# When SyncE waits for scatter-adds: ahead of all loads of a batch, or only ahead of the load of x

## The chip, the cores and the metric

The kernel runs on one core of one Trainium2 chip. The metric is the device time of one execution in microseconds (us); the time given for the kernel before is the median of three runs.

## The reference

One layer of a graph network over 100,000 nodes with 64 features and 25,000 edges:

```python
h = jnp.maximum(_layernorm(x), 0.0)
# src, dst: the two ends of each edge
msgs_f = mlp2(concat[h[src], h[dst], edge_attr], W1_f, b1_f, W2_f, b2_f)
agg    = segment_sum(msgs_f, dst)
msgs_r = mlp2(concat[h[dst], h[src], edge_attr], W1_r, b1_r, W2_r, b2_r)
agg    = agg + segment_sum(msgs_r, src)
out    = x + h + mlp2(concat[agg, h], Wn1, bn1, Wn2, bn2)
```

`mlp2` is two linear layers with a relu between them.

## The kernel before

Everything is float32. A table in device memory holds, for each node, the 128 values ahead of the node network's relu. Three stages work on it.

The first stage (to about 310 us) runs over 98 windows of 1024 nodes: it loads x, normalizes, multiplies by the lower part of Wn1 and stores the rows of the table. Meanwhile GpSimd (POOL) gathers rows of x for the ends of the edges, so that half of all gathers are done ahead of the second stage.

The second stage (about 340 to 1353 us) is the one that the change touches. It runs over 98 batches of 256 edges. A batch has four "tiles" of 128 edge ends. In its step n, each engine does this:

- DVE (`batch`, L1023): `aim` for batch n-2 (L1000, it writes the row numbers `scatter_at`, and first waits until the scatter-adds of batch n-4, which read the same buffer, have landed); `centre` for n+1; `match` for n-1 (L967, it compares `others`, the node numbers of all ends of the batch, with `ids`, and so finds ends that meet in the same node); `normal` for n; `targets` and `messages` for n-1; `add_h` for window n-1 (L1036, x + h).
- PE (`batch`, L850): `join` of n-2 (it sums messages of one node), `turn` of n (transposes `h_ends` and `edge_in`), `layer2` of n-1, `layer1` of n.
- ACT: root, relu, square, `copy_sums` of n-2 (the sums to `to_send`), and h of a window of nodes.
- POOL (`batch`, L570): `scatter` (L518) issues four indirect DMAs of 128 rows, which add `to_send` to rows of the table. It first waits until those of the batch before have landed. Then `gather_odd` (L535) issues two gathers of rows of x for a later batch.
- SyncE (SP, `batch`, L445): `behind_scatter` (L439) waits until the scatter-adds of batch n-4 have landed, the same landing on which `aim` waits. `load` (L353) loads `edge_in` (64 KB of edge features, L364) and twice `others` (128 KB each, the numbers spread to all partitions, L367) of batch n. It waits for its own buffers, `s_turn` and `s_same`, that is for `turn` and `match` of batch n-2. `load_x_edge` (L402) loads 256 KB of x for window n+2 (L385), and `store_xh` (L431) stores x + h of window n-1 (256 KB, L391), after waiting for DVE's `add_h` of that window.

Not all windows are stored: `in_ring` (L296) keeps some in SBUF. In each four windows, one is kept in the first 24 windows and two are kept after that, up to window 95; SP's step then ends with the load of x.

SP's queue runs in order, so whatever stands behind a wait waits as well. `behind_scatter` guards no buffer: it sets when SP's loads are issued. `s_loads_held` is a count on which nobody waits.

The third stage (to the end) loads the table and x + h, runs the rest of the node network and stores the output. It begins when all scatter-adds have landed.

Of the kernel before, what the change touches and what calls it, by code (L numbers as in the profile page):

```python
# [77 lines left out]
def gnn_layer(nc, x, src, dst, edge_attr, W1_f, b1_f, W2_f, b2_f, W1_r, b1_r, W2_r, b2_r, Wn1, bn1, Wn2, bn2, out):  # L78
# [39 lines left out]
    with ExitStack() as ctx:  # L118
# [205 lines left out]
        def _(sp):  # L324
# [106 lines left out]
            def store_xh(w, k):  # L431
                if not w.there(k) or not in_ring(w, k):
                    return
                i, s = w.of(2, k)
                sp.wait_ge(e_xh[s], i + 1)
                place = w.of(NRING, k)[1]
                store_window(out, i, s, flat(nxh[place]), e_stored[place])
# [5 lines left out]
                    sp.sem_inc(s_loads_held, 1)  # L443

            def batch(w):  # L445
                w.do(behind_scatter)
                if w.least() >= 2:
                    w.do(load)
                w.do(load_x_edge, 2, ring=NRING)
                store_xh(w, -1)  # L450

            run(sp, NB, [(4, MORE_FROM * NRING, 4), (MORE_FROM * NRING, 92, 4)], 1, batch)


# [710 lines left out]
```

## Time and profile before

| | us |
|---|---|
| median of the runs (1625.42 to 1633.73) | 1631.61 |
| the profiled execution | 1627.22 |
| its span, first to last instruction | 1625.5 |
| busy in the span: PE, PE weight loads, DVE | 1318.5, 997.1, 972.4 |
| busy in the span: ACT, POOL | 944.0, 1120.1 |
| POOL's scatter-adds, L532, 392 instructions | 640.9 |
| mean granted TensorE clock | 0.835 of full |

Times of instructions are those of the profiled execution. PE is TensorE's matmuls, PEld its weight loads, SPq the queue of SyncE, which only issues DMAs here. "Busy" of a POOL indirect DMA is the time in which POOL makes its descriptors; the data moves afterwards. The queue q0 (software dynamic) carries POOL's DMAs and q1 (hardware dynamic) those of SP; both run on the same 16 DMA engines.

### The profile page before, as it was taken

Reading aid. Unit: us, or ns where it says so; the run is one execution under the profiler, and the core shown is the slowest. Engines: PE = TensorE matmul, PEld = TensorE weight load, DVE = VectorE, ACT = ScalarE, POOL = GpSimd, SP = SyncE. Lnnn points to the kernel's source line nnn. Section 1 sums busy time; section 2 is a strip of 40 time slices with the busy share of each in tenths; the row PEclk is TensorE's granted clock in tenths of the full one; section 3 lists DMA queues with packets and bytes.
Section 4 is the critical chain, followed back from the end, with each engine's and each line's share of the span. In section 5 each row is a group of like instructions: output and inputs, shape, how many; then the busy total and the mean of one; then the engine's idle time right before and its main releaser. Section 6 shows DMA issues by size and latency. Waiting matters only on the chain.

```text
span 1625.5 us, 29085 instructions
## 1 busy us (share of the span) xinstructions
PE 1318.5 (81%) x7070; PEld 997.1 (61%) x7070; DVE 972.4 (60%) x2902; ACT 944.0 (58%) x2256; POOL 1120.1 (69%) x1003
## 2 busy tenths in 40 slices
PE   6988998457787788887877887878888865899998
PEld 4777776345565666665656665656666654666665
DVE  7999998336666666666665666666666641222222
ACT  5888888244555455555545555455555533677776
POOL 7899878888888888888888888888888862000000
PEclk9999999567878777778787778787777777999999
DMA  7999998335555555555545555555555546999998
GB/s 222 310 312 315 315 312 280 101 59 108 103 109 108 107 104 103 102 103 103 102 93 99 101 103 102 98 100 102 103 103 102 102 76 205 333 369 348 346 349 292
DMA packets 238374, 280.71 MB, mean 173 GB/s; under 512 B 53170, under 2 KB 155200, under 8 KB 238348
## 3 DMA queue, kind: packets, MB, share of 16 engines
q1 hardware_dynamic: 168408, 241.57, 44.7%
q0 software_dynamic: 68992, 38.59, 20.3%
q10 hardware_dynamic: 948, 0.30, 0.1%
q14 instruction: 21, 0.17, 0.0%
q8 instruction: 5, 0.08, 0.0%
HBM read 162.62 MB, written 117.72 MB: 172 GB/s over the span
## 4 chain that ended last, share of the span: by engine, by line
POOL 28%; issue 19%; DMA 15%; PE 9%; DVE 5%; ACT 1%; POOLq 0%; SPq 0%; DVEq 0%; another core or an unknown queue 0%; ACTq 0%
POOL table L532 24%; DMA out_x<-ncentred 12%; POOL got_odd L514 5%; DMA table<-to_send,scatter_at 3%; PE bank L846 3%; DVE ncentred L1137 2%; PE bank L820 2%; PE bank L818 2%; PE bank L833 1%; DVE same L979 1%; PE bank L871 1%; DMA same<-table 1%; PE bank L804 1%; PE bank L882 0%; DVE sums L961 0%
## 5 line engine op out<-in xcount | busy, mean ns | idle before, releaser
L532 POOL DMA_INDIRECT table<-to_send,scatter_at x392 | 640.9, 1635 | 134.1 <-issue 118.3
L846 PEld LDWEIGHTS bank<-message,same 128*128 128x128 f32 x1960 | 300.1, 243 | 47.1 <-issue 43.6
L846 PE MATMUL bank<-message,same 128*128 128x128 f32 x1960 | 322.4, 335 | 3.3 <-DVE message L1010 3.3
L639 ACT ACTIVATE nh<-nx,all_sums,all_rstd 128x64 f32<-128x64 f32 x784 | 280.2, 434 | 0.0
L514 POOL DMA_INDIRECT got_even<-in_x,gather_first x196 | 211.8, 1081 | 40.9 <-issue 36.1
L775 PE MATMUL bank<-wn_h,nturned 128*128 128x256 f32 x784 | 196.6, 394 | 26.9 <-ACT nhidden L683 18.4
L514 POOL DMA_INDIRECT got_odd<-in_x,gather_at x180 | 179.9, 999 | 54.8 <-issue 54.2
L818 PE MATMUL bank<-turned,w_ends 128*128 128x256 f32 x392 | 175.5, 540 | 37.8 <-ACT turned_edge L609 37.1
L804 PE MATMUL bank<-ident,h_ends 128*128 128x128 f32 x196 | 51.4, 355 | 184.4 <-DVE h_ends L1019 181.4
L1004 DVE TENSOR_TENSOR scatter_at<-moved,ids 128x4 int32<-128x4 f32 x98 | 16.0, 163 | 296.6 <-DMA table<-to_send,scatter_at 296.6
L775 PEld LDWEIGHTS bank<-wn_h,nturned 128*128 128x128 f32 x784 | 143.1, 192 | 63.3 <-issue 33.0
L820 PE MATMUL bank<-turned_edge,w_edge 64*128 64x256 f32 x392 | 179.4, 547 | 0.0
L991 DVE CUSTOM_DVE_ANT_0 junk<-same,earlier 128x128 bf16<-128x128 f32 (+3 forms) x392 | 168.9, 487 | 0.0
L713 ACT ACTIVATE nhidden<-bank,bn_col 128x512 f32<-128x512 f32 x196 | 124.0, 684 | 70.2 <-PE bank L871 70.2
L616 ACT ACTIVATE hidden<-bank,b 128x256 f32<-128x256 f32 x196 | 82.1, 470 | 124.3 <-PE bank L820 122.4
L979 DVE TENSOR_SCALAR same<-others,ids 128x128 f32<-128x128 int32 (+3 forms) x392 | 143.7, 429 | 11.7 <-issue 7.6
L804 PEld LDWEIGHTS bank<-ident,h_ends 128*128 128x128 f32 x196 | 28.9, 181 | 195.3 <-issue 195.3
L871 PE MATMUL bank<-ident,same 128*128 128x128 f32 x784 | 108.4, 282 | 38.1 <-DMA same<-table 36.5
L833 PE MATMUL bank<-w2n,hidden 128*128 128x128 f32 x784 | 139.0, 336 | 0.0
L625 ACT COPY to_send<-bank 128x512 f32<-128x512 f32 x98 | 56.6, 577 | 139.4 <-PE bank L846 55.7
L871 PEld LDWEIGHTS bank<-ident,same 128*128 128x128 f32 x784 | 85.4, 143 | 77.5 <-issue 53.7
L820 PEld LDWEIGHTS bank<-turned_edge,w_edge 64*128 64x128 f32 x392 | 75.1, 239 | 94.0 <-issue 94.0
(78 smaller groups left out, 1971.0 us busy)
## 6 DMA issues: line engine op xcount, KB each, us to landing
nx<-in_x SPq DMA_DIRECT2D x194, 256.0 KB
table<-nhidden SPq DMA_DIRECT2D x97, 512.0 KB
same<-table SPq DMA_DIRECT2D x97, 512.0 KB, 5.3
others<-numbers SPq DMA_DIRECT2D x196, 128.0 KB
out_x<-ncentred SPq DMA_DIRECT2D x97, 256.0 KB, 4.4
nx<-out_x SPq DMA_DIRECT2D x55, 256.0 KB, 4.6
out_x<-nh SPq DMA_DIRECT2D x31, 256.0 KB
table<-to_send,scatter_at POOLq DMA_INDIRECT x392
```

The lines of the kernel that those rows point to most:

```text
L514: pool.indirect_dma_start(to[:, k * D:(k + 1) * D], None, x, bass.IndirectOffsetOnAxis(ap=numbers[:, k:k + 1], axis=0)).then_inc(landed, 16)
L532: pool.indirect_dma_start(table, bass.IndirectOffsetOnAxis(ap=scatter_at[s][:, k:k + 1], axis=0), to_send[s][:, k, :], None, compute_op=AL ...
L639: last = act.activation(nh[s][:, g, :], nx[place][:, g, :], ACT.Relu, bias=all_sums[:, at, g:g + 1].rearrange("p a g -> p (a g)"), scale=a ...
L713: act.activation(nhidden[s][:, odd * 512:odd * 512 + 512], bank[2 + 2 * s + odd][:, :], ACT.Relu, bias=bn1_col[:, 0:1]).then_inc(n_hidden[ ...
L775: last = pe.matmul(bank[2 + 2 * s + half][:, c:c + 2 * M], nturned[s][:, q * P:(q + 1) * P], wn1_h[:, :, :].rearrange("p a m -> p (a m)"), ...
L818: pe.matmul(bank[2 + s][:, c:c + JT * P], w1_ends[:, end, :], turned[s][:, 0:JT * P], start=True, stop=False)
L820: last = pe.matmul(bank[2 + s][:, c:c + JT * P], w1_edge[:, end, :], turned_edge[s][:, :], start=False, stop=True)
L833: last = pe.matmul(bank[4 + s][:, k * M:(k + 1) * M], hidden[s][:, end, j * P:(j + 1) * P], w2n[:, end, :], start=True, stop=True)
L846: last = pe.matmul(bank[6 + s][:, k * M:(k + 1) * M], same[s][:, o, k * P:(k + 1) * P], message[s][:, o, :], start=(o == k), stop=(o == KB ...
L871: last = pe.transpose(bank[2 + 2 * s + odd][:, q * P:(q + 1) * P], ntab[place][:, g * M:(g + 1) * M], ident[:, :])
L979: last = dve.tensor_scalar(same[s][:, o, 0:w], row[:, 0:w], ids[s][:, o:o + 1], None, ALU.is_equal)
L991: last = dve.tensor_tensor_reduce(junk[s][:, k, 0:w], same[s][:, k, 0:w], earlier[:, KB * P - w:], 1.0, 0.0, ALU.mult, ALU.add, before[s][ ...
```

## The change

In SP's `batch` the wait for the landing changes its place with `load`. Nothing else changes.

```diff
             def batch(w):
-                w.do(behind_scatter)
                 if w.least() >= 2:
                     w.do(load)
+                w.do(behind_scatter)
                 w.do(load_x_edge, 2, ring=NRING)
                 store_xh(w, -1)
```

## Rows read from the trace of the kernel before

**Rows 1.** Busy time by stretch of the second stage; the columns are in the heading.
```profile
core 0: us, PE busy (x) PEld busy (x) DVE busy (x) ACT busy (x) POOL busy (x), PEclk, DMA share, GB/s
500.00:700.00 200.00, 163.13 (x773) 123.88 (x771) 126.51 (x454) 103.19 (x291) 164.96 (x116) 0.76 0.55 104
900.00:1100.00 200.00, 161.36 (x769) 122.27 (x768) 125.63 (x448) 101.86 (x288) 164.64 (x117) 0.77 0.54 101
```

**Rows 2.** Groups from 351.28 to 1295.70 us, 91 steps; busy, mean ns | idle before.
```profile
L532 POOL DMA_INDIRECT table<-to_send,scatter_at x364 | 595.8, 1637 | 111.3 <-issue 110.1 <-ACT to_send L625 1.2
L514 POOL DMA_INDIRECT got_odd<-in_x,gather_at x180 | 179.9, 999 | 54.8 <-issue 54.2 <-DMA table<-to_send,scatter_at 0.6
L1004 DVE TENSOR_TENSOR scatter_at<-moved,ids 128x4 int32<-128x4 f32 x92 | 15.1, 164 | 280.1 <-DMA table<-to_send,scatter_at 280.1
```

**Rows 3.** Timeline of a step with a store: start, us, engine, line.
```profile
797.06 0.10 SPq L364 DMA_DIRECT2D edge_in<-in_edge_attr  x1
797.75 1.75 POOL L532 DMA_INDIRECT table<-to_send,scatter_at  x1 [0.30 <-issue]
798.53 0.77 SPq L367 DMA_DIRECT2D others<-numbers  x2
799.38 0.35 SPq L385 DMA_DIRECT2D nx<-in_x  x1
802.55 0.68 DVE L1048 TENSOR_TENSOR nsquares<-nx,nh 128x512 f32<-128x512 f32 x1
803.26 0.37 SPq L391 DMA_DIRECT2D out_x<-nsquares  x1
803.58 1.55 POOL L532 DMA_INDIRECT table<-to_send,scatter_at  x1 [0.30 <-issue]
806.99 0.16 DVE L1004 TENSOR_TENSOR scatter_at<-moved,ids 128x4 int32<-128x4 f32 x1 [3.42 <-DMA table<-to_send,scatter_at]
808.05 1.75 POOL L532 DMA_INDIRECT table<-to_send,scatter_at  x1 [0.30 <-issue]
```

**Rows 4.** DMA queues from 805.13 to 806.50: packets, MB, share of 16 engines.
```profile
q0 software_dynamic: 141, 0.06, 53.8%
q1 hardware_dynamic: 16, 0.01, 2.4%
```

**Rows 5.** The same queues from 799.50 to 801.75.
```profile
q1 hardware_dynamic: 450, 0.28, 48.7%
q0 software_dynamic: 105, 0.05, 23.0%
```

**Rows 6.** Timeline of the step whose store came late.
```profile
409.10 1.57 POOL L532 DMA_INDIRECT table<-to_send,scatter_at  x1 [0.30 <-issue]
409.50 0.68 DVE L1048 TENSOR_TENSOR nh<-nx,nh 128x512 f32<-128x512 f32 x1
410.37 0.37 SPq L391 DMA_DIRECT2D out_x<-nh  x1
413.04 0.17 DVE L1004 TENSOR_TENSOR scatter_at<-moved,ids 128x4 int32<-128x4 f32 x1 [2.53 <-DMA table<-to_send,scatter_at]
413.94 1.75 POOL L532 DMA_INDIRECT table<-to_send,scatter_at  x1 [0.68 <-issue]
```

**Rows 7.** DMA queues from 411.00 to 412.75.
```profile
q1 hardware_dynamic: 144, 0.26, 45.2%
q0 software_dynamic: 152, 0.08, 42.1%
```

**Rows 8.** Stores of x + h by SP, count and first and last start.
```profile
L391 SPq DMA_DIRECT2D out_x<-nh x31: 343/368/374, 294.5 to 1321.6; - x31
L391 SPq DMA_DIRECT2D out_x<-nsquares x24: 356/368/376, 352.6 to 1301.3; - x24
```

**Rows 9.** Timeline without gathers, near the end of the stage.
```profile
1304.72 0.16 DVE L1004 TENSOR_TENSOR scatter_at<-moved,ids 128x4 int32<-128x4 f32 x1 [3.12 <-DMA table<-to_send,scatter_at]
1305.50 1.77 POOL L532 DMA_INDIRECT table<-to_send,scatter_at  x1 [2.54 <-DMA table<-to_send,scatter_at]
```

**Rows 10.** Timeline of a step in which DVE's L1048 and the fourth scatter-add meet.
```profile
824.27 0.68 DVE L1048 TENSOR_TENSOR nh<-nx,nh 128x512 f32<-128x512 f32 x1
824.39 2.00 POOL L532 DMA_INDIRECT table<-to_send,scatter_at  x1 [0.30 <-issue]
```

**Rows 11.** SP's queue: waits, us in total, times, longest; then who waits for `edge_in`.
```profile
SPq L443 <- DMA table<-to_send,scatter_at: 224.2, 42, 8.4
  ACT turned L608: 84.2, 53
  PEld bank L804: 52.0, 17
```

## The prediction

> **What bounds the kernel now.** I read the busy times by stretch first. In the second stage POOL is busy 165 of each 200 us, a little more than PE, which runs there at a granted clock of 0.76 [rows 1]. Busy shares that close decide nothing, so the groups come next. In the 91 steps from 351.28 to 1295.70 us (944.4 us, so 10.38 us a step) POOL has 364 scatter-adds of 1.637 us and 182 gathers of about 1.0 us, and its idle time ahead of them is nearly all "issue", the fixed 0.30 us between two instructions; only 1.8 us of it is a wait for anybody [rows 2]. So 4 x (1.64 + 0.30) + 2 x (1.00 + 0.30) = 10.4 us is the step: POOL runs through without a stop and sets the pace. PE and DVE have gaps; DVE alone stands 280 us in `aim`, waiting for scatter-adds to land [rows 2]. SP waits for the same landing [rows 11], but nobody on the path waits for SP: DVE has no wait for `others` among its costly ones, and the waits behind PE's `edge_in` transposes [rows 11] lie on ACT and PE, which have slack against POOL.
>
> The timeline of one step then shows how thin POOL's cover is. The fourth scatter-add is issued at 803.58 and its descriptors are made at 805.13; two gathers follow; DVE sees the landing at 806.99, that is 1.86 us later; the next batch's first scatter-add, which needs that landing, starts at 808.05, 2.92 us after 805.13 [rows 3]. The gap of 1.06 us between landing and start looks like slack, but most of it is not: where no gathers stand between, POOL starts 0.78 us after DVE's `aim` (1304.72 to 1305.50) [rows 9]. So the real slack is 1.06 - 0.78 = about 0.3 us a step. That is the number on which the change hangs.
>
> **The change part by part.** No instruction is added or removed. In each step three DMAs (64 + 2 x 128 KB) move in SP's queue from behind the wait for the landing to ahead of it. What then releases them is the end of SP's step before and the waits for their own buffers.
>
> *Steps behind a step without a store.* SP's step ends with the load of x, right after a landing; the edge loads then wait for `match` of two batches ago, which DVE does some 2.5 us after its `aim`. They go out while the first scatter-adds are made, where in the kernel before the load of x went (799.38) [rows 3]. The load of x goes out some 2.3 us earlier, at once after the landing. The fourth scatter-add, whose landing counts, moves alone as before. Cost: 0; what hides it is that landings of the first three scatter-adds are waited for only through the fourth.
>
> *Steps behind a store.* Here `turn` and `match` of the batch two back have long been done when SP gets past the store, which itself waited for DVE's L1048. In the kernel before SP stored at 803.26 and was then silent until 807.40 or so, after the landing; now it goes on to issue the edge loads at some 803.7 to 805.3. The store's 0.3 us ahead of the fourth scatter-add is typical: in the step shown, SP's store stands at 803.26 against 803.58 [rows 3]; over the stage the difference goes from -0.4 to +1.3 us with a median near 0. So the edge loads fall on the time in which the fourth scatter-add's data moves. Before, that time was empty: from 805.13 to 806.50 q0 moves 141 packets and q1 only 16 [rows 4]. I found q1 in that window in one step of 92.
>
> What does it cost to fill it? That one step is the nearest row. The store was issued at 410.37, late, and its 144 packets moved together with the fourth scatter-add, at 45% and 42% of the engines [rows 7]. The descriptors were made at 409.10 + 1.57 = 410.67 and the landing came at 413.04, 2.37 us later, against about 1.77 in the other steps (1.86 in rows 3): +0.6 us. And POOL's next scatter-add has an idle time of 0.68 instead of 0.30 us: +0.38 us on the path [rows 6]. That agrees with 0.6 - 0.3 of slack. The other end is the first scatter-add of a step, beside which the edge loads themselves move now: from 799.50, the end of its descriptors, to 801.75, 2.25 us, only 105 packets of q0 are through while q1 has 450 [rows 5], where the undisturbed fourth had 141 in 1.37 us [rows 4]. So edge loads, with many small packets (96 or more per us), hold a scatter-add up by over 0.9 us if they meet it whole; that would be 0.9 - 0.3 = 0.6 to 0.7 us of stall a step. The lower end: if the edge loads' data comes late (in rows 3 `others` is issued 1.5 us after `edge_in`), they meet only the tail, the delay stays under 0.3 us and costs nothing. I take the +0.38 us of the one step measured: the transfer is different but the meeting, a SP transfer over the fourth scatter-add, is the same, and the size lies between the ends.
>
> How often: 55 stores [rows 8], less those ahead of the first scatter-adds and the last two, behind which no edge loads come, leaves about 50. So 50 x 0.38 = 19 us, with ends 0 and 50 x 0.7 = 35 us.
>
> *DVE's phase.* DVE's step hangs on the landing, POOL's now in part too, so DVE shifts by 0.3 us against POOL in steps behind a delayed landing. POOL is sensitive to this: L1048 that ends 0.35 us ahead of the fourth scatter-add leaves it at 1.55 us [rows 3]; one that begins 0.12 us ahead of it makes it 2.00 us [rows 10]; one that begins 0.40 us behind it leaves it at 1.57 us [rows 6]. In the 92 steps, 25 fourth scatter-adds are long by over 0.1 us, 8.6 us together. A shift of 0.3 us takes some out and puts others in. The first scatter-add is 1.75 us where DVE's comparison starts after it and 1.64 where before, 0.1 us more in the shifted steps. I take 0.1 us a step, 50 x 0.1 = 5 us, with ends -9 (all 25 freed) and +20 (50 x 0.4).
>
> The Trainium skill speaks on both sides here. Its page "DMA: Bandwidth & Descriptors", section "Queues, rings and completion order", has each DMA engine take turns between the queues it has work for, a packet at a time; by that rule 45% against 42% is what two queues with work get, and the trace agrees [rows 7]. The same page's "Rules for kernel authors" advise to issue a DMA early and wait late, since its fixed cost then overlaps; by that rule the change is free or better, and the time stays at 1631 us. The rows on POOL's slack bear against it. On the phase, the page "SBUF — State Buffer", section "SBUF: two separate sides", says that a DVE instruction with two SBUF inputs and a GpSimd instruction exclude each other for a shared port pair, whichever starts first; rows 6 and 10 agree, L1048 having two SBUF inputs.
>
> Sum: 19 + 5 = 24 us. The profiled execution's 1627.2 would become 1651; the median of the runs shown is 4.4 us above it, so 1631.6 + 24 = 1655.6, say 1655 us. Differences under 0.5% (8 us) can't be told from no change.
>
> **The rivals.**
> - *Hidden after all.* The edge loads come so late or move so thinly that the landing slips by less than 0.3 us; the gathers cover it. For it: q1's `others` packets move at a third to a half of the engines' time, and half of the steps aren't touched. Against it: rows 5. Time 1628 to 1637, about 1632.
> - *Full meeting.* The landing slips by 0.9 us or more, as rows 5 show for the first scatter-add, and DVE's shift puts L1048 onto the fourth one: 50 x (0.65 + 0.3) = 47, up to 1631.6 + 47 = 1679.
> - *Faster, by phase.* The landing slips by less than 0.3 us, POOL loses nothing, and DVE's L1048, which in 25 steps begins up to 0.3 us ahead of the fourth scatter-add, moves behind its start, as in rows 6. Decides from: a shift of over 0.1 to 0.3 us in those steps without the clean ones moving in. Price: at most 8.6 us, 1623. Against it: most clean steps have L1048 ending within 0.4 us ahead of that start, so they'd move in.
> - *It doesn't do what it says.* The buffers' own waits hold the edge loads as long as the landing did. In no step as long by the timeline: behind a store `match` was done some 5 us before, and in the others the hold ends some 7 us ahead of the next landing. It would give 1631, inside the first rival.
>
> **How the numbers follow.** Forecast (a meeting at the size of rows 6, 1640 to 1666): 0.55. Full meeting, 1666 to 1680: 0.18. Hidden: 0.21. Faster by phase, 0.06, of which half is over 8 us. So slower 0.74, same 0.23, faster 0.03. The range leaves out the faster case and the ends of the others: 1630 to 1676.
>
> **What would show it.** In the changed trace: the edge loads of half of the steps within 0.5 us behind a store, with q1 busy while the fourth scatter-add moves; the time from the fourth scatter-add's end to DVE's L1004 2.3 to 2.7 us in those steps and 1.8 in the others; POOL's idle ahead of its first scatter-add 0.6 to 0.9 us in them, so a wait "DMA table" or "issue" that grows by 15 to 35 us over the stage; steps of 10.8 and 10.3 us in turn; first and third stage unchanged. Wrong would be: landings at 1.8 us everywhere (then it is hidden), or slower with landings unchanged (then DVE's phase alone did it). The steadiness of the meeting is what could fail: SP's place against POOL depends on DVE, and DVE on PE's clock.

## The result and the profile after

| | before | after |
|---|---|---|
| median of the runs, us | 1629.58 (1625.42 to 1633.73) | 1661.72 (1658.86 to 1670.3) |
| the profiled execution, us | 1627.22 | 1662.97 |
| its span, us | 1625.5 | 1661.2 |
| mean granted TensorE clock | 0.835 | 0.836 |

The changed kernel is slower, by a ratio of 1.0206 with a 95% interval of 1.0158 to 1.0254, or 32 us. All of it lies in the second stage: from POOL's first scatter-add to its last it takes 35 us more in the profiled executions. POOL carries the loss. Two groups of the changed kernel's page (busy us, mean ns | idle us ahead of them, what ended most of it):

```profile
L532 POOL DMA_INDIRECT table<-to_send,scatter_at x392 | 651.8, 1663 | 158.0 <-issue 122.8
L514 POOL DMA_INDIRECT got_odd<-in_x,gather_at x180 | 179.9, 999 | 54.9 <-issue 54.9
```

The same two groups of the kernel before, on its page:

```profile
L532 POOL DMA_INDIRECT table<-to_send,scatter_at x392 | 640.9, 1635 | 134.1 <-issue 118.3
L514 POOL DMA_INDIRECT got_odd<-in_x,gather_at x180 | 179.9, 999 | 54.8 <-issue 54.2
```

The gathers are the same. The scatter-adds have 158.0 - 134.1 = 23.9 us more idle time ahead of them and take 651.8 - 640.9 = 10.9 us longer; together 34.8 us, against 35.7 us by which the span grew. So two rows of a page account for the loss: two thirds are waits, one third longer instructions.

The changed kernel's busy times by stretch, to set beside [rows 1]:

```profile
core 0: us, PE busy (x) PEld busy (x) DVE busy (x) ACT busy (x) POOL busy (x), PEclk, DMA share, GB/s
500.00:700.00 200.00, 149.66 (x744) 115.18 (x743) 122.50 (x441) 98.83 (x278) 160.52 (x112) 0.79 0.56 103
900.00:1100.00 200.00, 160.93 (x760) 122.63 (x760) 122.02 (x438) 100.39 (x283) 162.78 (x114) 0.76 0.55 99
```

112 instead of 116 POOL instructions fit into the first of these stretches, and no engine is busier there than before: the sign of a pace-setting engine that now waits. The granted clock of TensorE went from 0.76 to 0.79 in the first stretch and from 0.77 to 0.76 in the second, so it isn't the cause.

Where POOL waits, a step with a store shows (timeline of the changed kernel: start, us, engine, line):

```profile
669.26 0.37 SPq L391 DMA_DIRECT2D out_x<-nh  x1
669.46 1.57 POOL L532 DMA_INDIRECT table<-to_send,scatter_at  x1 [0.30 <-issue]
669.88 0.39 SPq L364 DMA_DIRECT2D edge_in<-in_edge_attr  x1
670.45 0.96 SPq L367 DMA_DIRECT2D others<-numbers  x2
672.65 0.98 POOL L514 DMA_INDIRECT got_odd<-in_x,gather_at  x1 [0.30 <-issue]
674.59 0.17 DVE L1004 TENSOR_TENSOR scatter_at<-moved,ids 128x4 int32<-128x4 f32 x1 [5.19 <-DMA table<-to_send,scatter_at]
674.84 0.35 SPq L385 DMA_DIRECT2D nx<-in_x  x1
675.42 1.76 POOL L532 DMA_INDIRECT table<-to_send,scatter_at  x1 [1.78 <-DMA table<-to_send,scatter_at]
```

It answers to [rows 3]. The edge loads go out 0.6 us behind the store, while POOL still makes the descriptors of the fourth scatter-add (ready at 669.46 + 1.57 = 671.03). DVE sees the landing 3.56 us after that, not 1.86, and POOL's next scatter-add stands 1.78 us instead of 0.30. The DMA queues of the changed kernel in the stretch from 671.64 to 673.00, while that scatter-add's data moves:

```profile
q1 hardware_dynamic: 238, 0.11, 30.8%
q0 software_dynamic: 49, 0.02, 26.5%
```

In the same length of time q0 had moved 141 packets undisturbed [rows 4]; beside 238 packets of SP's it moves 49. From the point of the step at which [rows 4] begin, the end of the descriptors, the contrast is larger: from 671.03 to 672.40 q1 moves 405 packets and q0 only 6.

The meeting isn't the same in each step. A step of the changed kernel with a milder one:

```profile
733.64 0.68 DVE L1048 TENSOR_TENSOR nsquares<-nx,nh 128x512 f32<-128x512 f32 x1
733.68 2.07 POOL L532 DMA_INDIRECT table<-to_send,scatter_at  x1 [0.30 <-issue]
734.36 0.37 SPq L391 DMA_DIRECT2D out_x<-nsquares  x1
735.45 0.39 SPq L364 DMA_DIRECT2D edge_in<-in_edge_attr  x1
736.03 0.95 SPq L367 DMA_DIRECT2D others<-numbers  x2
737.78 0.16 DVE L1004 TENSOR_TENSOR scatter_at<-moved,ids 128x4 int32<-128x4 f32 x1 [3.12 <-DMA table<-to_send,scatter_at]
738.67 1.67 POOL L532 DMA_INDIRECT table<-to_send,scatter_at  x1 [0.30 <-issue]
```

Here the store comes 0.68 us behind the start of the fourth scatter-add, the edge loads 1.1 us behind the store, and the landing only 2.03 us behind the descriptors; POOL doesn't wait. But the scatter-add itself takes 2.07 us, since L1048 began 0.04 us ahead of it.

I worked the averages out from such rows of the timeline, for 90 steps. The first of them begins at 350.74 us and the last at 1305.54 us in the changed kernel, at 351.28 and 1275.32 us in the one before. "Landing" is from the end of the fourth scatter-add's descriptors to DVE's L1004; "next start" is from the same point to POOL's next scatter-add.

| mean over steps, us | landing | next start | step |
|---|---|---|---|
| before, 50 with a store | 1.75 | 2.92 | 10.43 |
| before, 40 without | 1.78 | 2.91 | 10.32 |
| after, 50 with a store | 2.49 | 3.36 | 10.92 |
| after, 40 without | 1.85 | 2.93 | 10.52 |

The 50 steps with a store fall into kinds. In 19 the store is issued earlier than 0.2 us behind the start of the fourth scatter-add: the landing takes 3.03 us on average and the next start 3.87. In the 31 others the landing takes 2.16 us on average. In all, 29 of the 50 stand longer than before and 21 don't. The 90 steps are 32.5 us longer: 22.5 us in the time to the next start and 10 us in longer scatter-adds (33 instead of 25 fourth ones are long by over 0.1 us, and the first and third ones are a little longer on average).

### The profile page after: what moved, and what is told of

Read it like the earlier page. It is cut to its first block, busy times and chain, and to the rows that moved or that the text cites. A ratio compares the mean times of both kernels' runs of the same rounds, so it can differ in the third digit from the quotient of the medians.

```text
span 1661.2 us, 29085 instructions
## 1 busy us (share of the span) xinstructions
PE 1313.0 (79%) x7070; PEld 995.4 (60%) x7070; DVE 972.3 (59%) x2902; ACT 945.0 (57%) x2256; POOL 1131.1 (68%) x1003
## 4 chain that ended last, share of the span: by engine, by line
POOL 35%; issue 21%; DMA 17%; PE 3%; DVE 2%; POOLq 0%; SPq 0%; ACT 0%; DVEq 0%
POOL table L532 28%; DMA out_x<-ncentred 11%; POOL got_odd L514 6%; DMA table<-to_send,scatter_at 5%; DVE ncentred L1137 2%; PE bank L871 1%; PE bank L882 1%; PE bank L846 1%; DMA same<-table 1%; PE bank L892 0%; SPq L391 0%; PE bank L820 0%; PE bank L818 0%; PE bank L833 0%; DVE same L979 0%
## 5 line engine op out<-in xcount | busy, mean ns | idle before, releaser
L532 POOL DMA_INDIRECT table<-to_send,scatter_at x392 | 651.8, 1663 | 158.0 <-issue 122.8
L846 PEld LDWEIGHTS bank<-message,same 128*128 128x128 f32 x1960 | 286.4, 234 | 47.0 <-issue 41.4
L846 PE MATMUL bank<-message,same 128*128 128x128 f32 x1960 | 308.1, 325 | 5.4 <-DVE message L1010 5.4
L804 PE MATMUL bank<-ident,h_ends 128*128 128x128 f32 x196 | 55.7, 380 | 223.2 <-DVE h_ends L1019 218.1
L1004 DVE TENSOR_TENSOR scatter_at<-moved,ids 128x4 int32<-128x4 f32 x98 | 16.0, 163 | 313.8 <-DMA table<-to_send,scatter_at 313.8
L818 PE MATMUL bank<-turned,w_ends 128*128 128x256 f32 x392 | 170.0, 524 | 23.0 <-ACT turned_edge L609 23.0
L820 PE MATMUL bank<-turned_edge,w_edge 64*128 64x256 f32 x392 | 171.2, 524 | 0.0
L833 PE MATMUL bank<-w2n,hidden 128*128 128x128 f32 x784 | 147.2, 350 | 0.0
L833 PEld LDWEIGHTS bank<-w2n,hidden 128*128 128x128 f32 x784 | 139.3, 266 | 2.2
```

The costliest lines, as they stand in the source:

```text
L532: pool.indirect_dma_start(table, bass.IndirectOffsetOnAxis(ap=scatter_at[s][:, k:k + 1], axis=0), to_send[s][:, k, :], None, compute_op=AL ...
L818: pe.matmul(bank[2 + s][:, c:c + JT * P], w1_ends[:, end, :], turned[s][:, 0:JT * P], start=True, stop=False)
L820: last = pe.matmul(bank[2 + s][:, c:c + JT * P], w1_edge[:, end, :], turned_edge[s][:, :], start=False, stop=True)
L833: last = pe.matmul(bank[4 + s][:, k * M:(k + 1) * M], hidden[s][:, end, j * P:(j + 1) * P], w2n[:, end, :], start=True, stop=True)
L846: last = pe.matmul(bank[6 + s][:, k * M:(k + 1) * M], same[s][:, o, k * P:(k + 1) * P], message[s][:, o, :], start=(o == k), stop=(o == KB ...
```

## The experiments

Theory 1 is the meeting: edge loads that follow a store move while the fourth scatter-add does, it lands late, and POOL waits. Theory 2 is the phase: only DVE's place against POOL has changed. Theory 3 blames the load of x, which now goes out directly behind the landing.

**The change in half of the steps.** `e1_behind_no_store` loads ahead of the wait only where the step of SP before ended without a store:

```diff
+                early = w.there(-2) and not in_ring(w, -2)
+                if early:
+                    w.do(load)
                 w.do(behind_scatter)
-                if w.least() >= 2:
+                if w.least() >= 2 and not early:
                     w.do(load)
```

> The edge loads go ahead of the wait for the landing only in steps of SP that follow a step without a store (42 of 92); behind a store the order is the old one. Theory 1 (meeting: edge loads that follow a store run over the data of the fourth scatter-add, it lands late and POOL waits): no meeting is left, so the time is that of the kernel before, 1629 us within 8, with DVE's row L1004 1.75 to 1.85 us behind the end of the fourth scatter-add in all steps. Theory 2 (phase: only DVE's place against POOL has changed, by the new order of the loads, and long scatter-adds make the loss): part of the loss stays, some 40 of 90 steps, +10 to +15 us. Theory 3 (the load of x, which now goes out 2.3 us earlier, is what hurts): it goes out early in the steps touched, so about half of the loss, +15 us.

Measured: 1629.54 us, ratio 0.9997 (0.9979 to 1.0015): no loss, with a mean landing of 1.8 us in both kinds of step. `e2_behind_store` is the same without the `not`:

> The other half: the edge loads go ahead of the wait only in steps of SP that follow a store (50 of 92). Theory 1 (meeting): the whole loss of the changed kernel, +25 to +35 us, so 1655 to 1665; the landing behind a store 2.5 us after the fourth scatter-add on average against 1.8. Theory 2 (phase) and theory 3 (early load of x): about half of it, +15 us.

Measured: 1658.51 us, ratio 1.0176 (1.0151 to 1.0201): nearly the whole loss, with a mean landing of 2.41 us behind a store. The groups of POOL's scatter-adds, first of `e1_behind_no_store`:

```profile
L535 POOL DMA_INDIRECT table<-to_send,scatter_at x392 | 642.7, 1640 | 134.5 <-issue 118.4 <-DMA table<-to_send,scatter_at 15.1 <-ACT to_send L628 0.9
```

and of `e2_behind_store`:

```profile
L535 POOL DMA_INDIRECT table<-to_send,scatter_at x392 | 654.3, 1669 | 154.5 <-issue 121.0 <-DMA table<-to_send,scatter_at 33.5
```

The first has nearly the idle time and the busy time of the kernel before, the second nearly those of the changed one. Theory 3 would have split the loss, and theory 2 had put 10 to 15 us on the first of the two; neither came. The phase has a price, as `e6_before_add_first` will show, but this change reaches it only by way of late landings.

**The change without the meeting.** `e3_store_late` keeps the changed order in every step, and holds the store back behind the next landing:

```diff
                 w.do(load_x_edge, 2, ring=NRING)
-                store_xh(w, -1)
+                store_xh(w, -2)
```

(with one more step at the end of the loop).

> The changed kernel, with each store of x + h held back one step further: it is issued behind the load of x of the next step, so behind the landing. SP's step then ends with something that is never later than the landing plus 1 us in every step, and the edge loads of all steps wait for the comparison of two batches ago, some 2.5 us behind the landing. Theory 1 (meeting): nothing of SP moves while the fourth scatter-add does; landings at 1.8 us, time 1629 us within 8, so the whole loss is gone though the edge loads still go ahead of the wait in every step. Theory 3 (the load of x goes out at once behind the landing): the loss stays, about 1660. Theory 2 (phase): anything between, with landings unchanged.

Measured: 1628.29 us, ratio 0.9988 (0.9973 to 1.0003). The loss is gone with the load of x still directly behind the landing. A step of `e3_store_late`:

```profile
695.29 0.37 SPq L364 DMA_DIRECT2D edge_in<-in_edge_attr  x1
695.83 0.94 SPq L367 DMA_DIRECT2D others<-numbers  x2
699.24 1.57 POOL L532 DMA_INDIRECT table<-to_send,scatter_at  x1 [0.31 <-issue]
702.49 0.16 DVE L1004 TENSOR_TENSOR scatter_at<-moved,ids 128x4 int32<-128x4 f32 x1 [3.12 <-DMA table<-to_send,scatter_at]
702.72 0.34 SPq L385 DMA_DIRECT2D nx<-in_x  x1
703.76 0.72 SPq L391 DMA_DIRECT2D out_x<-nh  x1
```

The edge loads are 4 us ahead of the fourth scatter-add, and the landing comes 1.68 us behind its descriptors.

**Which of the loads.** `load` is split into `load_features` (`edge_in`) and `load_numbers` (both `others`), and only one goes ahead of the wait. `e4_features_ahead`:

```diff
                 if w.least() >= 2:
-                    w.do(load)
+                    w.do(load_features)
                 w.do(behind_scatter)
+                if w.least() >= 2:
+                    w.do(load_numbers)
```

> Only edge_in, the 64 KB of edge features (256 packets), goes ahead of the wait; both loads of others (512 packets, 256 KB) stay behind it. Theory 1 (meeting): edge_in alone holds the engines for some 0.3 us behind the store; it delays the landing behind a store by 0.1 to 0.3 us, which POOL's 0.3 us of slack mostly covers: 1630 to 1640 us. Theory 2 and 3: theory 3 expects no loss here, since the load of x stays as late as before; theory 2 expects up to +8 us either way with landings at 1.8 us.

Measured: 1630.18 us, ratio 1.0005 (0.9992 to 1.0018), with a mean landing of 1.87 us behind a store. `e5_numbers_ahead` has the two in the other order:

> Only others, the two loads of 128 KB (512 packets), go ahead of the wait; the load of edge_in stays behind it. Behind a store, others now moves some 0.6 us sooner after the store than in the changed kernel. Theory 1 (meeting): others are what holds the fourth scatter-add up, so most of the loss of the changed kernel or all of it is there, +20 to +40 us, landings of 2.3 to 3.5 us behind a store. Rival 4 (it takes the number of SP's DMAs, or all 320 KB): about a half, +10 to +15 us.

Measured: 1691.61 us, ratio 1.0376 (1.0353 to 1.04): 62 us lost, beyond the expectation of theory 1 (up to 40), and twice the loss of the change itself. Moving less ahead cost more. Without `edge_in` in front, `others` is issued 1.33 us behind the start of the fourth scatter-add on average, not 1.80, and in 49 of the 50 steps POOL's next start is late, not in 29: the mean landing behind a store is 2.99 us, the next start 3.82 us. The group of the scatter-adds in `e5_numbers_ahead`:

```profile
L539 POOL DMA_INDIRECT table<-to_send,scatter_at x392 | 656.4, 1675 | 180.5 <-issue 115.5 <-DMA table<-to_send,scatter_at 63.8 <-ACT to_send L632 1.2
```

**DVE's phase, and the meeting made whole.** DVE's `add_h` (L1048) goes ahead of `messages`, so that it no longer waits for PE; the store comes about 1 us sooner. `e6_before_add_first` does this to the kernel before:

```diff
-                w.do(messages, -1)
                 add_h(w, -1)
+                w.do(messages, -1)
```

> The kernel before, with DVE's add_h ahead of messages in each step, so that L1048 doesn't wait for PE and begins behind the start of the third scatter-add and ends ahead of the fourth; SP's store comes about 1 us earlier. Theory 1 says nothing new here: no edge loads meet the landing, it stays at 1.8 us. Theory 2 (phase) puts its price: the 25 long fourth scatter-adds (8.6 us in all) go, so 1620 to 1629 us; if the third one gets long instead, it is the same as before.

Measured: 1619.12 us, ratio 0.9939 (0.9919 to 0.9958). A step of `e6_before_add_first`:

```profile
632.48 1.56 POOL L532 DMA_INDIRECT table<-to_send,scatter_at  x1 [0.30 <-issue]
632.65 0.69 DVE L1048 TENSOR_TENSOR nsquares<-nx,nh 128x512 f32<-128x512 f32 x1
633.37 0.37 SPq L391 DMA_DIRECT2D out_x<-nsquares  x1
634.34 1.55 POOL L532 DMA_INDIRECT table<-to_send,scatter_at  x1 [0.30 <-issue]
```

L1048 begins 0.17 us behind the start of the third scatter-add, which stays at 1.56 us, and has ended a microsecond ahead of the fourth. None of the 90 fourth ones is long any more. In the profiled executions all scatter-adds together are 6.3 us shorter than in the kernel before; the rest of the 10 us is not traced to a row. `e7_after_add_first` is the same edit on the changed kernel:

> The changed kernel, with the same move of add_h. The store, and with it the edge loads behind it, comes about 1 us earlier against the fourth scatter-add, so the edge loads meet it whole in every step behind a store. Theory 1 (meeting): every such landing is like the worst ones of the changed kernel, 3.0 to 3.5 us, POOL stands 0.8 to 1.3 us more in 50 steps: 1670 to 1695 us. Theory 2 (phase: long fourth scatter-adds make the loss): the loss gets smaller, 1625 to 1650 us.

Measured: 1677.85 us, ratio 1.0291 (1.0271 to 1.0311). This separates the two theories best: the edit that makes the kernel before 10 us faster makes the changed kernel 16 us slower. The group of `e7_after_add_first` from its page:

```profile
L532 POOL DMA_INDIRECT table<-to_send,scatter_at x392 | 637.6, 1627 | 187.1 <-issue 122.4
```

Its scatter-adds are 14.2 us shorter than in the changed kernel, its idle time ahead of them is 29.1 us longer. The store now comes early in every step, and so do the edge loads; the landings behind a store take 2.74 to 3.49 us. In the changed kernel itself 9 of the 50 took over 3.13 us, the longest 3.87 us, so the delay hangs on where in the scatter-add's time the loads fall, and this kernel's mean isn't its upper bound.

`e8_both` puts `add_h` first in `e3_store_late`:

> The changed kernel with the store held back behind the next landing, as in e3_store_late, and add_h ahead of messages. Theory 1: no SP transfer near the fourth scatter-add and no long fourth ones, so as e6_before_add_first or a little better: 1618 to 1628 us, a version that is faster than both kernels. Rival: the long ones move to the third scatter-add, 1629 us.

Measured: 1621.28 us, ratio 0.9946 (0.9929 to 0.9964). It is 0.5% faster than the kernel before, which is clear of noise, like `e6_before_add_first`, and not better than that one: the early edge loads bring nothing of their own.

**What sets the size of the delay.** Three kernels put different loads ahead of the wait, all with `add_h` first, so that the meeting comes early in each step behind a store. `e9_x_ahead_add_first`:

```diff
+                w.do(load_x_edge, 2, ring=NRING)
                 w.do(behind_scatter)
                 if w.least() >= 2:
                     w.do(load)
-                w.do(load_x_edge, 2, ring=NRING)
```

> As e6_before_add_first, but the load of x (256 KB in 128 packets of 2 KB) goes ahead of the wait for the landing and the edge loads stay behind it. Behind a store it meets the fourth scatter-add whole. The question is what sets the size of the delay. If it is the bytes or the time that the engines need (256 KB, about 0.8 us of all 16 engines, near to that of both others), the landing is 1.2 us late as in e5 and e7, and the time is 1665 to 1680 us. If it is the number of packets, it is about a half or less: landing 0.5 to 0.6 us late as in rows 6, POOL stands some 0.3 us in 50 steps, 1632 to 1642 us.

Measured: 1636.89 us, ratio 1.0048 (1.0032 to 1.0064), or 18 us above `e6_before_add_first`, the kernel to compare it with, since both have `add_h` first. `e10_one_number_add_first` splits `load_numbers` by end (`load_one` is the first of the two loads, `load_rest` is `edge_in` and the second):

```diff
-                    w.do(load)
+                    w.do(load_one)
                 w.do(behind_scatter)
+                if w.least() >= 2:
+                    w.do(load_rest)
```

> As e6_before_add_first, but one of the two loads of others (128 KB in 256 packets) goes ahead of the wait, the other and edge_in stay behind it. By the number of packets: half of the delay of both, landing 0.6 to 0.7 us late, 1635 to 1645 us. By a fixed price of any load with such packets that meets the scatter-add: as with both, 1665 us or more.

Measured: 1637.89 us, ratio 1.005 (1.0037 to 1.0064), 19 us above `e6_before_add_first`. `e11_both_numbers_add_first` is `e5_numbers_ahead` with the edit of `add_h`:

> As e5_numbers_ahead with add_h ahead of messages: both loads of others (256 KB in 512 packets) ahead of the wait, edge_in behind it, the meeting as early as it gets. The whole-meeting price for 512 packets: landing 3.0 to 3.3 us, 1670 to 1682 us. It would be less only if they now pass ahead of the scatter-add's data in part: then landing below 2.8 us, 1650 to 1665 us.

Measured: 1665.1 us, ratio 1.021 (1.0173 to 1.0246); the landing of 2.86 us is between the two cases expected, and the time is at the edge of the lower one. Means over the steps with a store, worked out as above:

| ahead of the wait, `add_h` first | KB, packets | landing, us | next start, us |
|---|---|---|---|
| nothing (`e6_before_add_first`) | 0 | 1.75 | 2.92 |
| x (`e9_x_ahead_add_first`) | 256, 128 | 2.31 | 3.13 |
| one of `others` (`e10_one_number_add_first`) | 128, 256 | 2.30 | 3.13 |
| both of `others` (`e11_both_numbers_add_first`) | 256, 512 | 2.86 | 3.68 |
| `edge_in` and both (`e7_after_add_first`) | 320, 768 | 3.13 | 3.95 |

Three readings. First, the same 256 KB delay the landing by 0.56 us as 128 large packets and by 1.11 us as 512 small ones, and half of the small ones do as much as all the large ones: neither bytes nor packets alone give the size. Second, two other measures fit better, and no run here separates them. One is the number of loads ahead of the wait: one load gives 0.56 or 0.55 us, two give 1.11 us, three give 1.38 us. The other, more roughly, is the time that the packets take on the engines. A packet of 2 KB takes 84 ns, one of 512 bytes 27 ns and one of 256 bytes 18 ns (medians of these traces); the count times this, spread over 16 engines, is an estimate of 0.67, 0.43, 0.86 and 1.15 us for the four lower rows, against delays of 0.56, 0.55, 1.11 and 1.38 us. Third, the next start is 0.82 us behind the landing in each of the four lower rows, and 1.17 us in the first: POOL begins at 2.92 us or 0.82 us behind the landing, whichever is later, so the slack is 2.10 - 1.75 = 0.35 us.

The queues of `e9_x_ahead_add_first` from 682.85, the end of the descriptors, to 684.70, and then those of `e7_after_add_first` from 701.46 to 703.80, likewise:

```profile
q0 software_dynamic: 181, 0.08, 44.9%
q1 hardware_dynamic: 138, 0.25, 36.4%
```

```profile
q1 hardware_dynamic: 552, 0.23, 42.9%
q0 software_dynamic: 133, 0.06, 30.9%
```

Beside 2 KB packets q0 has 181 packets through in 1.85 us, beside small ones 133 in 2.34 us.

## Why the prediction was right, and where not

The time was 1661.7 us, forecast 1655, inside the range; the kernel is slower, as forecast, by 32 us and not 24.

- *POOL sets the pace and the slack is about 0.3 us a step.* Right. The last table gives 0.35 us, and every later landing costs its excess one to one.
- *Steps behind a step without a store cost nothing.* Right: `e1_behind_no_store`. SP's waits of the changed kernel show the hold that was foreseen, the edge loads waiting for `match`:

```profile
SPq L358 <- DVE same L979: 76.1, 37, 2.5
```

- *Steps behind a store meet the fourth scatter-add.* Right in place: `e2_behind_store` holds the loss, `e3_store_late` removes it. But the fourth scatter-add's data did not move alone before in every step. In 22 others of the 92 steps, 40 to 75 of q1's packets, the store's, began within 1.37 us of the end of the fourth scatter-add's descriptors, and it landed after 1.62 to 1.80 us all the same. The step of [rows 6] had 69 such packets and a landing of 2.38 us; its store was the latest of all. And the edge loads of [rows 5] move 450 packets in 2.25 us, which is 200 per us where I wrote 96 or more.
- *50 x 0.38 = 19 us of stall.* The sum was near (22.5 us in 90 steps, 0.44 us a step behind a store), but not for the reason given. The row from which I took it, the late store of [rows 6], is a meeting with 128 packets of 2 KB. Measured whole, such a meeting delays by 0.56 us (`e9_x_ahead_add_first`), and [rows 6] were a good row for that. The edge loads, early in each step, delay by 1.38 us and make POOL stand 1.03 us longer (`e7_after_add_first`), beyond the 0.9 us, and the stall of 0.6 to 0.7 us, that I had put as the upper end from [rows 5]. What brought the mean down again is that only 19 of 50 steps met them early. Two errors, in size and in share, partly cancelled, so it is luck that the stall came near. A whole meeting in each step was the second rival. Its 1679 us is close to the 1677.9 us of `e7_after_add_first`, but by chance too: the rival charged 33 us of stall and 15 us of phase, where that kernel has 52 us of stall and starts from one that is 10 us faster.
- *0.1 us a step for DVE's phase, 5 us.* Mis-sized: 10 us. The steps that follow a late landing, mostly those without a store, are 0.2 us longer (10.52 against 10.32 us) where I had charged 0.1, and 33 instead of 25 fourth scatter-adds are long.
- *Left out:* the last steps of the stage, which have no gathers as cover. A late landing there lies on the path whole. The rest of the stage behind the 90 steps is 2.7 us longer.
- *The shared port, rows 6 and 10.* Half of what I read there is shown. L1048 makes a scatter-add long when it starts first; when the scatter-add starts first, neither is held up: L1048 takes 0.68 us in [rows 6] as in [rows 10], though the scatter-add beside it in [rows 6] is busy for 1.17 us after L1048 begins.
- *The idle time would grow by 15 to 35 us* (23.9) *and the first and third stage stay* (they did). Steps of 10.8 and 10.3 us in turn came as 10.9 and 10.5 on average, far from regular; that the meeting isn't steady was named as what could fail.

The Trainium skill's page "DMA: Bandwidth & Descriptors", in "Queues, rings and completion order", has an engine take turns between queues a packet at a time. What it calls a packet is a bundle of descriptors, while the 128 rows of a 256 KB load are 128 packets in the profile's count, so the table can't test the rule, and neither can the near shares of [rows 7]; no run here shows the turns themselves. The advice of the same page's "Rules for kernel authors", to issue a DMA early, speaks of the transfer that is moved; here nobody on the path waited for that transfer, and it cost another one its cover. That DMAs run on the same engines and interleave "regardless of the engine that started them" (section "Issuing engines are not separate DMA queues") is in line with the runs: SP's loads delay POOL's scatter-adds.

## What to carry to other kernels

Before a transfer is moved up, look at what moves on the DMA engines at its new place, and whether something on the pacing engine waits for that. A wait that guards no buffer may still do work: here it kept SP's small-packet loads off the one scatter-add in four whose landing is waited for with 0.35 us to spare. And what precedes a step in a queue decides as much as what is in it: the same loads were free behind a step without a store and cost all of the loss behind one with a store.

## What the runs showed of the hardware

- Loads from SP that move beside an indirect scatter-add of 128 rows delay its landing by 0.56 us (256 KB in 2 KB packets), 0.55 us (128 KB in 512-byte packets), 1.11 us (256 KB in 512-byte packets) and 1.38 us (with 64 KB in 256-byte packets on top), on average in the kernels with `add_h` first.
- `edge_in` alone, 64 KB in 256 packets, in front of the others, seems to act as a spacer, since `others` is then issued 0.47 us later: with it the loss was 32 us, without it 62 us. That the later issue is the reason was not tested by itself.
- L1048, a DVE instruction with two SBUF inputs, makes a scatter-add's descriptors late only if it starts first: 2.07 us where it began 0.04 us ahead, 1.56 us where it began 0.17 us behind. L1048 itself takes 0.68 us in either case. Moving that one instruction brought 10 us (0.6%) to the kernel before.
